# Comparisons of place in edge bucketing: six of the 34 rows made by ScalarE as a rectified one less the squared distance

## The chip, the cores and the metric

The kernel runs on one core of a Trainium2 chip. The metric is the device time of one execution in microseconds; the time of a kernel is the median of its runs. In the profile PE is TensorE (PEld its weight loads), DVE is VectorE, ACT is ScalarE, POOL is GpSimd, and SP is the engine that issues most DMAs.

## The reference

Four graph layers follow one another on 6250 nodes with 96 features and 100000 edges (`src`, `dst`, sorted by `dst`), each as x + layer(relu(layernorm(x))): four-head attention over edges, a softmax-weighted sum of messages, ten steps of a propagation, and two graph convolutions. All of them sum over edges by node. The cut below shows the shape of the work.

```python
edge_index = jnp.stack([src, dst])
h = jnp.maximum(_layernorm(x, axis=-1), 0.0)
x = x + _L0_gnn_ref(h, L0_gnn_qW, L0_gnn_kW, L0_gnn_vW, src, dst)   # exp(q.k) weights, segment_sum by src
h = jnp.maximum(_layernorm(x, axis=-1), 0.0)
x = x + _L1_gnn_ref(h, src, dst, L1_gnn_W, L1_gnn_b)                # softmax over dst, segment_sum, linear
h = jnp.maximum(_layernorm(x, axis=-1), 0.0)
x = x + _L2_gnn_ref(h, edge_index)                                   # ten times: out = A out * 0.9 + h * 0.1
h = jnp.maximum(_layernorm(x, axis=-1), 0.0)
x = x + _L3_gnn_ref(h, edge_index, L3_gnn_W1, L3_gnn_b1, L3_gnn_W2, L3_gnn_b2)
```

## The kernel before

The kernel turns the edge list into a dense adjacency matrix in tiles of 128 nodes, and does every sum over edges as a matmul. Its stages in time are: loads and the first norm; **bucketing** of the edges (`bucket_edges`); attention together with the writing of the adjacency; then the dense layers, which stream the adjacency back and are the rest of the span.

Bucketing, the stage that is changed, runs over 25 groups of 256 destination nodes. A group has its edges in 128 partitions of `RUN` = 34 each ("rows" r = 0 to 33, handled in 17 pairs, `TWOS_RUN`). For each edge it finds the rank among the edges of the group that have the same source tile (49 tiles), and puts the edge's code in the slot (rank, tile). One turn of the loop does this:

- PE, `tensor_rank` (L944): 83 small matmuls sum the rank of each edge of group g in the bank `rank_ps` (`pr`, 34 columns). 49 of them take the slices of `prod`, one for each tile.
- ACT (L979) copies `pr` into `rank`, as bf16.
- DVE, `vector_place` (L862): compares `rank` with 0 to 127 and writes the one-hot `onerank`, 128 columns for each of 34 rows. It does so in three instructions, of 6, 6 and 5 pairs, and signals `hot_r` after each.
- PE, `tensor_place` (L954): 34 matmuls, `onerank` of a row against `vals` of it, summed in `po`. It waits for `hot_r` before rows 0, 12 and 24 (`third` = 12), and signals `placed`.
- ACT (L990) copies `po` into the column g of `placed`, and signals `slots_out`.

Around this lie, for the group after it, the counting (`tensor_count`, L930, and ACT's copy of it, `before`, L984, which DVE's `prod`, L852, needs) and the projection of two node tiles to q, k, v: PE transposes (L623), ACT copies them to `aT` (L631), PE multiplies (`q_out`, L639), ACT takes the high half (L652) and DVE the low half (L659).

The order on each engine is that of the program. A turn is on PE: rank of g, count and transposes of g + 1, place of g, products of g + 1. On ACT: `rank`, `before`, `aT`, `placed`, then the two high halves. On DVE: `prod`, `bt`, `near`, `far`, `vals`, two low halves, three of `onerank`. Turn 20 also loads the Exp table on ACT, in turn 21 DVE decodes the first 20 groups (`decode(0)`, L805 to L815), and turn 25, the last, has place only.

Of the kernel before, what the change touches and what calls it, by code (L numbers as in the profile page):

```python
# [5 lines left out]
ALU = mybir.AluOpType  # L6
ACT = mybir.ActivationFunctionType
AX = mybir.AxisListType
F32, F16, BF16, F8 = mybir.dt.float32, mybir.dt.float16, mybir.dt.bfloat16, mybir.dt.float8e4
I32, U16, U8 = mybir.dt.int32, mybir.dt.uint16, mybir.dt.uint8  # L10

P = 128
# [5 lines left out]
GROUPS = -(-NODES // GROUP)  # L18
# [3 lines left out]
RUN = 34  # L22
# [15 lines left out]
EARLY = (CHUNKS - 1) * CHUNK  # L38
TURN = (6, BTILES // 2)
BANK = 4  # L40
AHEAD = 3
UP = -(-GROUPS // BANK)
HOMES = 5
# [70 lines left out]
def over(ap, n):  # L114
    return ap.unsqueeze(2).to_broadcast([ap.shape[0], ap.shape[1], n])
# [14 lines left out]
def signals(k):  # L130
    k.spare = k.sig("spare")
    k.const_raw, k.consts, k.ident_b = k.sig("const_raw"), k.sig("consts"), k.sig("ident_b")
    k.x_zero, k.dall_in, k.x_in, k.params_in = (k.sig(x) for x in ("x_zero", "dall_in", "x_in", "params_in"))
    k.below, k.first_ps, k.first, k.edges_in, k.edges_in2 = (
        k.sig(x) for x in ("below", "first_ps", "first", "edges_in", "edges_in2"))
    k.ln_x, k.ln_sum, k.ln_mean, k.ln_cen, k.ln_sq, k.ln_var, k.ln_vare, k.ln_std, k.ln_rstd, k.ln_h = (
        k.sig(x) for x in ("ln_x", "ln_sum", "ln_mean", "ln_cen", "ln_sq", "ln_var", "ln_vare", "ln_std", "ln_rstd",
                           "ln_h"))
    k.lin_tr, k.lin_copied, k.lin_mm, k.lin_out = (k.sig(x) for x in ("lin_tr", "lin_copied", "lin_mm", "lin_out"))
    k.x_plus, k.q_unit, k.q_unit_ps, k.q_root, k.q_scaled, k.q_per, k.q_hi, k.q_lo = (  # L140
        k.sig(x) for x in ("x_plus", "q_unit", "q_unit_ps", "q_root", "q_scaled", "q_per", "q_hi", "q_lo"))
    k.bound_in, k.eps_in = k.sig("bound_in"), k.sig("eps_in")
    k.rows_t, k.rows_sb, k.kv_zero = (k.sig(x) for x in ("rows_t", "rows_sb", "kv_zero"))
    k.rows_out = [k.sig(f"rows_out{h}") for h in range(2)]
    k.prepared = k.sig("prepared")
    k.bt, k.val, k.counted, k.before, k.same, k.prod, k.ranked, k.rank, k.hot_r, k.placed, k.slots_out = (
        k.sig(x) for x in ("bt", "val", "counted", "before", "same", "prod", "ranked", "rank", "hot_r", "placed",
                           "slots_out"))
    k.codes, k.decoded, k.planes = k.sig("codes"), k.sig("decoded"), k.sig("planes")
    k.base1, k.full_s, k.full_ps, k.filled_s = (k.sig(x) for x in ("base1", "full_s", "full_ps", "filled_s"))  # L150
    attention_signals(k)
    k.most_s, k.most_ps, k.verdict = (k.sig(x) for x in ("most_s", "most_ps", "verdict"))
# [528 lines left out]
def bucket_edges(k, ctx, edges, projection):  # L681
# [23 lines left out]
    far = [k.buf(ctx, f"far{i}", [P, 2, FAR, 2 * FAR], BF16) for i in range(2)]  # L705
    before = [k.buf(ctx, f"before{i}", [P, TILES, 2], BF16) for i in range(2)]
    rank = k.buf(ctx, "rankb", [P, RUN], BF16)
    onerank = k.buf(ctx, "onerank", [P, TWOS_RUN, P, 2], BF16)
    placed = k.buf(ctx, "placed", [P, BTILES, GROUPS], BF16)
    parts = ((0, EARLY), (EARLY, GROUPS))  # L710
# [14 lines left out]
    pr = k.bank(ctx, "rank_ps")  # L725
    pp = [k.bank(ctx, f"pp{i}") for i in range(2)]
    po = k.bank(ctx, "po")
    third = 2 * -(-TWOS_RUN // 3)
    tile1 = tile0[:, :, RUN:]

    def in_twos(row, n):
# [11 lines left out]

    def vector():
        v.tensor_scalar(count0_2[:], over(k.count1[:], 2), 1.0, None, ALU.subtract)
        v.tensor_copy(number_2[:], over(k.count1[:, 0:TILES], 2))
        v.tensor_copy(identh[:], k.ident[:])
        v.memset(placed[:, TILES:BTILES, :], 0.0)
        starts.count()
        starts.place()  # L750
        for turn in range(BODIES + AHEAD):
            if turn < BODIES:
                norm.center(turn)
            if turn == 0:
                projection.squares()
            elif turn == 1:
                projection.roots()
            elif turn == AHEAD:
                projection.units()
            if turn >= AHEAD:  # L760
                norm.scale(turn - AHEAD)
        prepare()
        for turn in range(GROUPS + 1):
            if turn:
                vector_before(turn - 1)
            if turn < GROUPS:
                vector_count(turn)
            if turn:
                projection.low(turn - 1)
                if turn == GROUPS:  # L770
                    planes(0)
                vector_place(turn - 1)
            if turn == EARLY + 1:
                decode(0)
        decode(1)
        planes(1)
        v.wait_ge(k.full_ps.sem, k.full_ps.at(1))
        v.tensor_reduce(k.filled[:], pc[0:1, 0:2], AX.X, ALU.add).then_inc(k.filled_s.sem, 1)
# [76 lines left out]
    def vector_place(g):  # L855
        v.wait_ge(k.rank.sem, k.rank.at(g + 1))
        if g:
            v.wait_ge(k.placed.sem, k.placed.at(g))
        ranks = in_twos(rank[:], P)
        for r0 in range(0, TWOS_RUN, third // 2):  # L860
            r1 = min(r0 + third // 2, TWOS_RUN)
            v.tensor_tensor(onerank[:, r0:r1, :, :], count0_2[:].unsqueeze(1).to_broadcast([P, r1 - r0, P, 2]),  # L862
                            ranks[:, r0:r1, :, :], ALU.is_equal).then_inc(k.hot_r.sem, 1)

# [54 lines left out]
    def copy_rows(h, n0, n1, m):  # L919
        first = h * n_early  # L920
        a.wait_ge(k.rows_t.sem, k.rows_t.at(first + n1))
        a.activation(flat(k.slot_rows[0:m, first + n0:first + n1, :]), pt[h][0:m, 0:(n1 - n0) * P],
                     ACT.Copy).then_inc(k.rows_sb.sem, 1)
# [23 lines left out]
    def tensor_place(g):  # L947
        pe.wait_ge(k.val.sem, k.val.at(g + 1))
        if g:
            pe.wait_ge(k.slots_out.sem, k.slots_out.at(g))  # L950
        for r in range(RUN):
            if r % third == 0:
                pe.wait_ge(k.hot_r.sem, k.hot_r.at(3 * g + r // third + 1))
            t = pe.matmul(po[:, 0:TILES], onerank[:, r // 2, :, r % 2], vals[g % 2][:, r // 2, :, r % 2],  # L954
                          start=r == 0, stop=r == RUN - 1)
        t.then_inc(k.placed.sem, 1)

    def scalar():
        a.wait_ge(k.consts.sem, k.consts.at(1))
        a.activation(warm[:], k.ones[:, 0:1], ACT.Sqrt).then_inc(k.kv_zero.sem, 1)  # L960
        starts.load(a, range(0, BY_SCALAR), k.edges_in)
        a.wait_ge(k.eps_in.sem, k.eps_in.at(1))
        for turn in range(BODIES + 1):
            if turn < BODIES:
                norm.square(turn)
            if turn:
                norm.deviation(turn - 1)
            if turn == 1:
                projection.root()
        for i in range(2):  # L970
            a.activation(k.aT[i][D:D + 1, :].rearrange("o (j p) -> o j p", p=P), under(k.ones[D:D + 1, :], RING), ACT.Copy)
        a.wait_ge(k.x_plus.sem, k.x_plus.at(16 * BODIES))
        for turn in range(GROUPS + 1):
            g = turn - 1
            if turn:
                a.wait_ge(k.ranked.sem, k.ranked.at(g + 1))
                if g:
                    a.wait_ge(k.hot_r.sem, k.hot_r.at(3 * g))
                a.activation(rank[:], pr[:, 0:RUN], ACT.Copy).then_inc(k.rank.sem, 1)  # L979
            if turn < GROUPS:  # L980
                a.wait_ge(k.counted.sem, k.counted.at(turn + 1))
                if turn >= 2:
                    a.wait_ge(k.prod.sem, k.prod.at(turn - 1))
                a.activation(before[turn % 2][:], over(pp[turn % 2][:, 0:TILES], 2), ACT.Copy).then_inc(k.before.sem, 1)  # L984
                projection.copy(turn)
            if turn == EARLY:
                a.activation(warm[:], k.ones[:, 0:1], ACT.Exp).then_inc(k.kv_zero.sem, 1)
            if turn:
                a.wait_ge(k.placed.sem, k.placed.at(g + 1))
                a.activation(placed[:, 0:TILES, g:g + 1], po[:, 0:TILES].unsqueeze(2), ACT.Copy).then_inc(k.slots_out.sem, 1)  # L990
            if turn < GROUPS:
                projection.high(turn)
            i = turn - EARLY - 1
            if 0 <= 8 * i < n_early:
                n1 = min(8 * i + 8, n_early)
                copy_rows(0, 8 * i, n1, EARLY * min(TURN[0], BTILES - 4 * i * TURN[0]))
        copy_rows(1, 0, 4, CHUNK * TURN[1])

    def spread(h, n0, n1):

# [1480 lines left out]
```

## Time and profile before

| | us |
|---|---|
| median of three runs | 3947.27 (3946.36 to 3948.25) |
| the profiled execution's own time | 3949.03 |
| its span | 3947.6 |
| PE busy | 3852.8 (98%) |
| DVE busy | 1728.5 (44%) |
| ACT busy | 1305.7 (33%) |
| one steady turn of bucketing | 6.88 |

A row of the timeline gives the start in us from the span's start, how long it took, the engine, the line, and in brackets how long that engine had been idle before and what ended the wait. The chain is the work that ended last, followed backwards; what lies on it sets the time.

### The profile page before, as it was taken

The numbers are of one execution on the slowest core, as the hardware profiler recorded it, in microseconds if no ns is written. First come the engines' busy times: TensorE is split into PE (matmuls) and PEld (weight loads), VectorE is DVE, ScalarE is ACT, GpSimd is POOL, SyncE is SP. The second block draws the span as 40 slices with busy tenths as digits, with TensorE's granted clock in tenths as the row PEclk, the third lists the DMA queues.
The fourth block names the chain that finished last, engine by engine and source line by source line (L and its number), as shares of the span: only waits on it lengthen the run. The fifth ranks groups of instructions, "written<-read, shape, count | busy, mean of one in ns | idle before, by whom it ended". The sixth has DMA issues, their size and how long they took to land.

```text
span 3947.6 us, 124895 instructions
## 1 busy us (share of the span) xinstructions
PE 3852.8 (98%) x46633; PEld 3664.5 (93%) x46633; DVE 1728.5 (44%) x4347; ACT 1305.7 (33%) x3974; POOL 589.7 (15%) x724
## 2 busy tenths in 40 slices
PE   5899999999999999999999999999999998999999
PEld 4789999999956668999999999999999998999999
DVE  8999999999963234222222222222222222331211
ACT  3268888888831012222221222212222221111110
POOL 1046666666610000000000000000000000000000
PEclk9999999999999999999999999999999999999999
DMA  3069898998953334566666565555655655666775
GB/s 66 3 170 231 232 239 232 233 236 231 239 162 112 112 106 156 205 201 205 202 203 204 200 205 201 203 204 200 205 201 202 204 201 175 207 218 209 213 214 157
DMA packets 441659, 750.12 MB, mean 190 GB/s; under 512 B 201515, under 2 KB 333227, under 8 KB 441496
## 3 DMA queue, kind: packets, MB, share of 16 engines
q1 hardware_dynamic: 438826, 744.71, 62.0%
q0 software_dynamic: 1232, 2.65, 0.4%
q8 instruction: 128, 2.10, 0.2%
q10 hardware_dynamic: 1438, 0.37, 0.0%
q14 instruction: 35, 0.29, 0.0%
HBM read 621.77 MB, written 83.32 MB: 179 GB/s over the span
## 4 chain that ended last, share of the span: by engine, by line
PE 95%; DVE 2%; issue 1%; SPq 1%; ACT 1%; DMA 0%; POOL 0%; DVEq 0%; ACTq 0%; POOLq 0%
PE sum L1939 50%; PE sum L1553 20%; PE pk L1274 10%; PE pr L1297 7%; PE pq L1286 3%; PE pc L1310 2%; PE rank_ps L944 2%; PE l L521 1%; DVE onerank L862 1%; PE q_out L639 1%; PE l L505 0%; PE sum L1764 0%; PE po L954 0%; SPq L288 0%; SPq L183 0%
## 5 line engine op out<-in xcount | busy, mean ns | idle before, releaser
L1939 PE MATMUL sum<-u,ring 128*128 128x192 f16 x12005 | 993.8, 246 | 0.0
L1939 PEld LDWEIGHTS sum<-u,ring 128*128 128x128 fp8e4 x12005 | 992.6, 98 | 0.8 <-issue 0.6
L1939 PE MATMUL sum<-y,ring 128*128 128x192 f16 x11662 | 962.9, 246 | 0.0
L1939 PEld LDWEIGHTS sum<-y,ring 128*128 128x128 fp8e4 x11662 | 962.2, 98 | 0.0
L1553 PE MATMUL sum<-u,ring 128*128 128x385 f16 (+1 forms) x4802 | 607.5, 287 | 7.6 <-issue 4.6
L1553 PEld LDWEIGHTS sum<-u,ring 128*128 128x128 fp8e4 x4802 | 435.1, 98 | 169.3 <-issue 8.0
L1948 DVE TENSOR_TENSOR z<-lo,sum 128x96 f32<-128x96 f32 x441 | 112.2, 254 | 988.6 <-ACT lo L1963 988.0
L1274 PE MATMUL pk<-kv,hT 128*128 128x192 f16 x4900 | 486.0, 246 | 2.0 <-DVE hT L1166 2.0
L1274 PEld LDWEIGHTS pk<-kv,hT 128*128 128x128 f16 x4900 | 410.1, 99 | 2.4 <-DVE hT L1166 2.3
L1356 ACT ACTIVATE kvs<-pk 128x384 f32<-128x384 f32 x735 | 302.6, 436 | 111.6 <-PE pk L1274 94.9
L1963 ACT ACTIVATE lo<-sum 128x96 f32<-128x96 f32 x441 | 110.1, 250 | 654.9 <-PE sum L1939 654.6
L1297 PE MATMUL pr<-wv,hs_wide 128*128 128x101 f32 x2450 | 322.4, 279 | 2.0 <-POOL wv L1227 2.0
L1222 POOL TENSOR_SCALAR sc<-sc,bound 128x20 f32<-128x20 f32 x245 | 263.3, 1075 | 258.1 <-DVE sc L1150 258.1
L1297 PEld LDWEIGHTS pr<-wv,hs_wide 128*128 128x128 f32 x2450 | 293.9, 192 | 2.3 <-POOL wv L1227 2.3
L1227 POOL TENSOR_TENSOR wv<-kvs,wv 128x480 f32<-128x480 f32 x245 | 246.8, 1007 | 208.8 <-DVE hd L1197 136.8
L1553 PE MATMUL sum<-y,ring 128*128 128x192 f16 x2401 | 202.2, 246 | 0.0
L1553 PEld LDWEIGHTS sum<-y,ring 128*128 128x128 fp8e4 x2401 | 199.0, 98 | 0.1
L1329 ACT ACTIVATE row<-pc 128x512 uint16<-128x512 f32 (+1 forms) x343 | 185.5, 545 | 0.8
L1346 ACT ACTIVATE hs_wide<-hs 128x640 f32<-128x640 bf16 x245 | 180.1, 735 | 0.0
L1143 DVE TENSOR_TENSOR qk<-pq,kvs 128x480 f32<-128x480 f32 x245 | 160.3, 654 | 42.0 <-ACT kvs L1356 42.0
L1951 DVE SCALAR_TENSOR_TENSOR uf<-z,col_g,H 128x96 f32<-128x96 f32 x441 | 140.6, 319 | 80.9 <-DVE z L1948 80.9
L1166 DVE TENSOR_SCALAR hT<-rows,dpid 128x640 f16<-128x640 f16 x490 | 165.9, 380 | 0.0
(257 smaller groups left out, 3018.3 us busy)
## 6 DMA issues: line engine op xcount, KB each, us to landing
ring<-adjacency_t SPq DMA_DIRECT2D x490, 800.0 KB, 4.3
ring<-adjacency SPq DMA_DIRECT2D x147, 896.0 KB, 5.0
rows<-slot_rows_d SPq DMA_DIRECT2D x249, 320.0 KB, 3.9
adjacency<-row SPq DMA_DIRECT2D x49, 800.0 KB, 4.3
adjacency_t<-col SPq DMA_DIRECT2D x49, 800.0 KB, 4.5
col<-row SPq DMA_TRANSPOSE x245, 4.1
X<-H POOLq DMA_DIRECT2D x7, 336.0 KB, 3.9
X<-in_x_dram SPq DMA_DIRECT2D x6, 336.0 KB, 5.4
```

What stands on the lines that cost most here:

```text
L1143: v.tensor_tensor(qk[i][:].rearrange("p (g d) -> p g d", d=D), pq[i][:, 0:CHUNK * D].rearrange("p (g d) -> p g d", d=D), kv[i][:, :, 0:D], ...
L1166: t = v.tensor_scalar(halves(hT[i][:, 1 + m, :, :]), halves(rows[h][:, :, 1, :]), k.dpid[:, m:m + 1], None, ALU.is_equal)
L1222: pool.tensor_scalar(sc[i][:], sc[i][:], k.bound[:, 0:1], k.bound[:, 1:2], ALU.min, ALU.max).then_inc(k.clipped.sem, 1)
L1227: pool.tensor_tensor(wv[i][:, :, 0:D].rearrange("p g (h d) -> p g h d", d=DH), kv[i][:, :, D:2 * D].rearrange("p g (h d) -> p g h d", d=DH ...
L1274: t = pe.matmul(pk[n][:, place:place + 2 * D], hT[i][:, 1 + m, g, :], k.kv[:, 2 * (g0 + g) + m, part, :], start=m == part == 0, stop=m == ...
L1297: t = pe.matmul(pr[:, 0:AV], hs_wide[e % HOMES][:, g, :], wv[i][:, g, :], start=g0 + g == 0, stop=g0 + g == GROUPS - 1)
L1329: a.activation(flat(row[b][:, g:g + count, :]), pc[u % 2][:, 0:count * P], ACT.Copy, accum_out=rowsum[:, bass.ds(X * (2 * UP) + u, 1)]).th ...
L1346: a.activation(flat(hs_wide[e % HOMES][:]), hs[e % 2][:].rearrange("p g a t -> p (g a t)"), ACT.Copy).then_inc(k.wide.sem, 1)
L1356: a.activation(flat(kv[i][:, 2 * n:2 * n + count, :]), pk[n][:, 0:count * 2 * D], ACT.Copy).then_inc(k.kv_out.sem, 1)
L1553: t = pe.matmul(self.ps[j][:, 0:self.cols], w[:, q, (j + odd) // 2, :, (j + odd) % 2], U[:, r * RING + q, 0:self.cols], start=r == q == 0, ...
L1939: m = pe.matmul(ps[r][:, 0:2 * D], w[:, t // 2, :, t % 2], n["this"][:, t, 0:2 * D], start=t == 0, stop=t == TILES - 1)
L1951: v.scalar_tensor_tensor(uf[j][:], z[:, j, :], k.g[:, tile], flat(k.H[:, tile, :]), ALU.mult, ALU.add).then_inc(k.uf.sem, 1)
```

## The change

For each group, ScalarE makes the comparisons of the last six rows (28 to 33, `BY_SQUARES` = 6, three pairs); VectorE makes the other 28 (`by_vector` = 14 pairs, in instructions of 5, 5 and 4 pairs, `third` = 10). ScalarE first copies the six columns of `pr` as f32 into `rank_f`, then makes six Square instructions, (rank - count)^2, each with its own column of `rank_f` as bias, into `away`; and, after `before`, one Relu of 1 - `away` over all six rows, which reads `away` with the two rows of a pair interleaved and writes `onerank` in order. The value is 1 where count equals rank, else 0. PE waits for the new signal `hot_a` before row 28. How `rank_ps` is summed (all 49 slices) stays.

```diff
+BY_SQUARES = 6
@@ bucket_edges
+    rank_f = k.buf(ctx, "rank_f", [P, BY_SQUARES], F32)
+    away = k.buf(ctx, "away", [P, BY_SQUARES, P], BF16)
+    count0 = k.buf(ctx, "count0", [P, P], BF16)
...
-    third = 2 * -(-TWOS_RUN // 3)
+    by_vector = TWOS_RUN - BY_SQUARES // 2
+    third = 2 * -(-by_vector // 3)
@@ vector()
+        v.tensor_scalar(count0[:], k.count1[:], 1.0, None, ALU.subtract)
@@ vector_place
-        for r0 in range(0, TWOS_RUN, third // 2):
-            r1 = min(r0 + third // 2, TWOS_RUN)
+        for r0 in range(0, by_vector, third // 2):
+            r1 = min(r0 + third // 2, by_vector)
@@ tensor_place
-            if r % third == 0:
+            if r == 2 * by_vector:
+                pe.wait_ge(k.hot_a.sem, k.hot_a.at(g + 1))
+            elif r % third == 0 and r < 2 * by_vector:
@@ scalar()
+                a.activation(rank_f[:], pr[:, 2 * by_vector:RUN], ACT.Copy).then_inc(k.rank_f.sem, 1)
                 a.activation(rank[:], pr[:, 0:RUN], ACT.Copy).then_inc(k.rank.sem, 1)
+                scalar_away(g)
...
+            if turn:
+                scalar_place(g)
+            if turn < GROUPS:
                 projection.copy(turn)
...
+    def scalar_away(g):
+        a.wait_ge(k.rank_f.sem, k.rank_f.at(g + 1))
+        for r in range(BY_SQUARES):
+            x = a.activation(away[:, r, :], count0[:], ACT.Square, bias=rank_f[:, r:r + 1], scale=-1.0)
+        x.then_inc(k.away.sem, 1)
+
+    def scalar_place(g):
+        a.wait_ge(k.away.sem, k.away.at(g + 1))
+        if g:
+            a.wait_ge(k.placed.sem, k.placed.at(g))
+        a.activation(onerank[:, by_vector:, :, :], away[:].rearrange("p (a t) n -> p a n t", t=2), ACT.Relu,
+                     bias=k.ones[:, 0:1], scale=-1.0).then_inc(k.hot_a.sem, 1)
```

On ACT, one steady turn of bucketing before, from the copy of the rank to the high halves of the projection:

```order
64 L979 ACTIVATE rankb<-rank_ps 128x34 [waits hot_r,ranked]
65 L984 ACTIVATE before<-pp 128x98 [waits prod,counted]
66 L631 ACTIVATE aT<-q_turned 96x256 [waits lin_tr,lin_mm]
67 L990 ACTIVATE placed<-po 128x49 [waits placed]
68 L652 ACTIVATE H<-q_out 128x2x96 [waits lin_mm]
69 L652 ACTIVATE kv<-q_out 128x2x192
```

The same turn of ACT in the changed kernel:

```order
76 L988 ACTIVATE rank_f<-rank_ps 128x6 [waits hot_r,ranked]
77 L989 ACTIVATE rankb<-rank_ps 128x34
78 L1017 ACTIVATE away<-count,rank_f 128x128 [waits rank_f]
79 L1017 ACTIVATE away<-count,rank_f 128x128 x5
80 L995 ACTIVATE before<-pp 128x98 [waits prod,counted]
81 L1024 ACTIVATE onerank<-away,ones 128x768 [waits placed,away]
82 L633 ACTIVATE aT<-q_turned 96x256 [waits lin_tr,lin_mm]
83 L1004 ACTIVATE placed<-po 128x49 [waits placed]
84 L654 ACTIVATE H<-q_out 128x2x96 [waits lin_mm]
85 L654 ACTIVATE kv<-q_out 128x2x192
```

Eight instructions are new: `rank_f` stands ahead of the copy of the rank, six squares stand ahead of `before`, and the Relu into `onerank` stands between `before` and `aT`.

On PE, the place matmuls of a turn and the products after them, before:

```order
15 L954 MATMUL po<-vals,onerank 128x49 [waits hot_r,val]
16 L954 MATMUL po<-vals,onerank 128x49 x11
17 L954 MATMUL po<-vals,onerank 128x49 [waits hot_r]
18 L954 MATMUL po<-vals,onerank 128x49 x11
19 L954 MATMUL po<-vals,onerank 128x49 [waits hot_r]
20 L954 MATMUL po<-vals,onerank 128x49 x9
21 L639 MATMUL q_out<-wq_scaled,aT 128x288 [waits q_lo,lin_copied]
```

And the same place of PE in the changed kernel:

```order
15 L963 MATMUL po<-vals,onerank 128x49 [waits hot_r,val]
16 L963 MATMUL po<-vals,onerank 128x49 x9
17 L963 MATMUL po<-vals,onerank 128x49 [waits hot_r]
18 L963 MATMUL po<-vals,onerank 128x49 x9
19 L963 MATMUL po<-vals,onerank 128x49 [waits hot_r]
20 L963 MATMUL po<-vals,onerank 128x49 x7
21 L963 MATMUL po<-vals,onerank 128x49 [waits hot_a]
22 L963 MATMUL po<-vals,onerank 128x49 x5
23 L641 MATMUL q_out<-wq_scaled,aT 128x288 [waits q_lo,lin_copied]
```

The last six of the 34 matmuls got a wait of their own, for ACT's `hot_a`; the products behind them wait for `aT` (`lin_copied`), as before.

## Rows read from the trace of the kernel before

**Rows 1.** Busy time of each engine in bucketing, and in one steady turn.

```profile
core 0: us, PE busy (x) PEld busy (x) DVE busy (x) ACT busy (x) POOL busy (x), PEclk, DMA share, GB/s
44.00:220.00 176.00, 153.81 (x3871) 134.85 (x3872) 168.72 (x256) 50.81 (x153) 0.00 (x0) 0.98 0.05 13
108.45:115.33 6.88, 6.11 (x165) 5.36 (x161) 6.70 (x11) 1.94 (x6) 0.00 (x0) 1.00 0.02 5
```

**Rows 2.** The chain that ended last, one turn: start us, us, what.

```profile
110.98 0.21 ACT rankb L979
...
112.96 0.83 DVE onerank L862
...
113.83 0.44 PE po L954 x10
114.27 1.06 PE q_out L639 x4
115.33 2.50 PE rank_ps L944 x83
```

**Rows 3.** The timeline of the same turn, DVE, ACT and PE.

```profile
110.98 0.20 ACT L979 ACTIVATE rankb<-rank_ps 128x34 bf16<-128x34 f32 x1 [1.78 <-PE rank_ps L944]
111.21 2.56 DVE L862 TENSOR_TENSOR onerank<-count,rankb 128x1536 bf16<-128x1536 bf16 x3 [0.18 <-ACT rankb L979]
...
111.87 0.25 ACT L984 ACTIVATE before<-pp 128x98 bf16<-128x98 f32 x1 [0.69 <-PE pp L930]
112.18 0.38 ACT L631 ACTIVATE aT<-q_turned 96x256 f32<-96x256 f32 x1
...
113.69 1.02 DVE L852 TENSOR_TENSOR prodb<-bt,before 128x1666 bf16<-128x1666 bf16 x1
113.83 0.33 PEld L954 LDWEIGHTS po<-vals,onerank 128*128 128x128 bf16 x10 [0.35 <-DVE onerank L862]
...
114.09 0.78 PEld L639 LDWEIGHTS q_out<-wq_scaled,aT 96*128 96x128 f32 x4
...
117.36 0.55 DVE L659 TENSOR_TENSOR kv<-q_out,kv 128x384 f16<-128x384 f32 x1
```

**Rows 4.** Groups by line and shape, 40 to 420 us: the comparisons on DVE.

```profile
L862 DVE TENSOR_TENSOR onerank<-count,rankb 128x1536 bf16<-128x1536 bf16 x50 | 45.7, 955 | 6.5 <-ACT rankb L979 6.5
...
L862 DVE TENSOR_TENSOR onerank<-count,rankb 128x1280 bf16<-128x1280 bf16 x25 | 20.5, 818 | 0.0
```

**Rows 5.** Groups of ACT by line and shape over the whole span.

```profile
L312 ACT ACTIVATE T<-H 128x672 f32<-128x672 f32 x21 | 16.0, 763 | 115.5 <-DVE H L307 115.5
...
L222 ACT ACTIVATE T<-H 128x96 f32<-128x96 f32 x49 | 13.1, 267 | 7.1 <-DVE H L215 7.1
...
L990 ACT ACTIVATE placed<-po 128x49 bf16<-128x49 f32 x25 | 9.8, 393 | 42.9 <-PE po L954 42.9
...
L979 ACT ACTIVATE rankb<-rank_ps 128x34 bf16<-128x34 f32 x25 | 5.0, 199 | 44.4 <-PE rank_ps L944 44.4
...
L228 ACT ACTIVATE col<-col,eps 128x7 f32<-128x7 f32 x7 | 1.9, 285 | 0.0
```

**Rows 6.** ACT's timeline in the first norm: two small instructions, back to back.

```profile
15.59 0.28 ACT L228 ACTIVATE col<-col,eps 128x7 f32<-128x7 f32 x1
15.78 0.19 ACT L592 ACTIVATE q_unitb<-q_unitb 128x3 f32<-128x3 f32 x1
```

**Rows 7.** The timeline of turn 0, where the products waited for `aT`.

```profile
43.76 0.38 ACT L631 ACTIVATE aT<-q_turned 96x256 f32<-96x256 f32 x1 [0.15 <-PE q_turned L623]
44.19 1.46 PEld L639 LDWEIGHTS q_out<-wq_scaled,aT 96*128 96x128 f32 x4 [0.90 <-ACT aT L631]
```

**Rows 8.** DVE's timeline at the start: one instruction that reads every 16th element.

```profile
5.17 0.21 DVE L262 CAST some<-dall 125x50 f32<-125x50 int32 x1 [0.35 <-DMA dall<-in_edges_dram]
```

**Rows 9.** The timeline of turn 21, behind `decode(0)`.

```profile
193.72 1.02 DVE L852 TENSOR_TENSOR prodb<-bt,before 128x1666 bf16<-128x1666 bf16 x1
...
194.81 0.53 PEld L944 LDWEIGHTS rank_ps<-near,identb 128*128 128x128 bf16 x16
```

**Rows 10.** The chain ahead of bucketing.

```profile
29.79 4.10 DMA edges<-in_edges_dram
```

More of the change, by code:

```diff
@@ L148, in signals @@
                            "slots_out"))
+    k.rank_f, k.away, k.hot_a = (k.sig(x) for x in ("rank_f", "away", "hot_a"))
     k.codes, k.decoded, k.planes = k.sig("codes"), k.sig("decoded"), k.sig("planes")
```

## The prediction

> **What bounds the kernel now.** I read the busy time by stretch first. In bucketing DVE is busy 168.72 of 176 us and PE 153.81, ACT only 50.81; in one steady turn of 6.88 us DVE works 6.70, PE 6.11, ACT 1.94 [rows 1]. So DVE looks like the bound and ACT has 4.9 us a turn to spare. Then the chain of waits, which says what a turn really hangs on [rows 2]: the 83 rank matmuls (2.50), ACT's copy of the rank (0.21), the three DVE comparisons, the last ten place matmuls (0.44), the products (1.06), and the rank matmuls again. Everything else of DVE fits beside this, with 0.18 us to spare: that is its idle time before `onerank` [rows 3]. So both a DVE instruction in `onerank` and an ACT or PE instruction between rank and products are on the path. Last the timeline of that turn [rows 3]. I call T the end of the rank matmuls (110.96, which is 0.02 ahead of ACT's copy) and give places as T plus so much: `rank` copied T+0.02 to T+0.22, `onerank` T+0.25 to T+2.81, `before` from T+0.91, `aT` T+1.22 to T+1.60, the last place weights at T+2.87, the products' first weights at T+3.13. From there to the next T is 6.88 - 3.13 = 3.75, work of PE alone that the change doesn't touch.
>
> **What comes off DVE.** Six pairs of rows take 0.955, five 0.818 [rows 4]: 0.137 a pair, and the three pairs that leave are worth 0.41 a turn. On the path that is the whole gain there is: 25 turns x 0.41 = 10.3 us, 0.26% of the kernel.
>
> **What comes ahead of the copy of the rank.** `rank_f` is a copy of 6 columns. ACT's price is a fixed part and 0.86 ns an element ((763 - 267) / (672 - 96), [rows 5]); 28 columns less than the 199 ns of `rank` make 0.175. Two ACT instructions overlap by 0.09: the one of 0.28 at 15.59 is followed at 15.78 [rows 6]. So `rank` starts 0.08 later, and `onerank` runs from T+0.33 to T+2.48. Of the 0.41 there is 0.33 left. The third DVE piece is now followed by 8 + 6 matmuls in place of 10, at 0.026 each (the ten take from 113.83 to 114.09, [rows 3]), which takes 0.10 more. If ACT's part were there in time, the products would start at T+2.90, 0.23 earlier than now.
>
> **What ACT has to do first.** A 128x96 Square takes 0.267 without a tensor as bias [rows 5]. A bias tensor costs about 0.09: 0.285 for 7 elements with one, 0.19 for 3 without [rows 5, 6]. So one square of 128 elements is 0.267 + 32 x 0.00086 + 0.09 = 0.385, and the next starts 0.295 after it. The squares start at T+0.21 (after `rank`), the last of six at T+0.21 + 5 x 0.295 = T+1.69, and it ends at T+2.07. `before`, due at T+0.91 now, starts at T+1.98 and ends at T+2.23. It is queued behind the squares, and DVE's `prod` waits for it, but `prod` stands behind `onerank`, which ends at T+2.48: covered by 0.25. The Relu starts 0.16 after `before`, at T+2.14. It does 768 elements with a bias tensor: 0.763 + 96 x 0.00086 + 0.09 = 0.94 if its read costs no more than a plain one, so `hot_a` comes at T+3.08. Behind it on ACT is `aT`, for which the products on PE wait: it starts at T+2.14 + 0.94 - 0.09 = T+2.99, takes 0.38, ends at T+3.37, and PE loads 0.05 after its end (43.76 + 0.38 to 44.19, [rows 7]). **Products at T+3.42**, against T+3.13: a steady turn gets 0.29 us longer, 7.17. The six last place matmuls (T+3.13 to T+3.29) hide under `aT`. DVE gets off the path (6.29 of 7.17 busy), PE waits more.
>
> **The price of the Relu's read** is what the trace doesn't show: it takes turns between two rows 256 bytes apart, and no ACT row here reads like that. Lower bound: the plain 0.94. Upper bound: the one ACT row whose access jumps, the 49 scattered elements of `placed`, at 0.393 [rows 5]; less a fixed 0.17 (199 ns less 34 x 0.86) that is 4.5 ns an element, and the Relu would be 768 x 0.0045 + 0.26 = 3.7 us. But there it is the write that jumps, while the Relu writes in order. A read that jumps is in one row, on DVE: 50 elements, each 64 bytes from the last, in 0.21 [rows 8], no more than such small instructions take anyway. It is the nearest row, so I take the plain price.
>
> In a sentence apart: the Trainium skill (SBUF — State Buffer, its note on cachelines) says that SBUF has lines of 16 bytes, that at least two hits in a line are needed for full bandwidth, and that each access that crosses to a new line pays; by that rule every element of this read pays, which is the second rival below, and the DVE row of 64-byte steps speaks against it (it shows another engine).
>
> **The turns that differ.** Turns 1 to 20, 22 and 23 are steady: 22 x 0.29 = 6.4. Turn 21 has `decode(0)` on DVE behind `onerank`, and PE's rank starts at 194.81, just after `prod` (193.72 + 1.02) [rows 9]: there DVE's 0.33 are a gain, and ACT's work is under the decode, -0.3. Turn 24 projects one tile, `aT` is 0.1 shorter: +0.2. Turn 25 has neither `before` nor `aT`; ACT ends at T+3.0, about when DVE's path did: 0. The `count0` instruction at the start is covered, since DVE then waits for a DMA of edges that lands at 33.9 [rows 10]. Attention after bucketing is untouched and starts as much later. Turn 20's table load stands behind `aT` and ahead of `placed`, where ACT has over a microsecond.
>
> **The sum:** 6.4 - 0.3 + 0.2 = +6.2 us (rounded), to be set against the profiled execution's own 3949.03, which gives 3955.3; that execution lies 1.8 over the median of the runs, so I state it against the median: 3947.27 + 6.2 = **3953.5**, 0.16% more. A measurement of this kernel can tell about 0.2% (7.9 us) from no change, so the forecast falls under "same", with 0.07 us a turn to the border.
>
> **Rivals.**
>
> *The intended gain.* If ACT's chain ends before DVE's, the products start at T+2.90. That needs `aT` by T+2.85, 0.52 sooner than I sum, so squares at an interval of 0.21 instead of 0.295, which would be so if the bias tensor cost nothing. Then it's 22 x -0.23, -0.3 in turn 21 and -0.4 in the last two: -5.8, **3941.5**. For it: 6.70 of DVE's 6.88 busy. Against it: the 0.285 for seven elements. Even this rival isn't over 0.2%.
>
> *The jumping read costs extra* (ends on the other side). Each 0.07 us more in the Relu makes the kernel measurably slower, since it is on the path in 24 turns (all but 21). At half speed, 0.86 ns more an element, the Relu takes 1.60, each turn 0.66 more: 6.2 + 24 x 0.66 = +22, **3969**. This is the likely form of the rule named above. For it: the alternation is with every element, and `placed` shows that ACT can pay for a jump. Against: the DVE row.
>
> *The jump costs what the write of `placed` does,* 3.7 us: 2.8 more in 24 turns, +67 and 6.2, **4021**. PE would wait 3 us a turn and might lose clock too. Against: it is a row of single 2-byte writes.
>
> *The change does less than it says* can't be: the order shows all eight new ACT instructions in each turn, and no further table load.
>
> **Chances.** Forecast (ACT's path ends last, plain read, +3 to +10) 0.55; the gain 0.12; extra read cost up to 1 us a turn 0.24; more 0.09. Of the forecast's 0.55 I give 0.15 to over 7.9 us, for small waits between dependent ACT instructions that I set at nothing (0.07 a turn decides). So faster by over 0.2%: 0.02, within 0.2%: 0.50, slower: 0.15 + 0.24 + 0.09 = 0.48. The range reaches from the gain to the half-speed read, 3941 to 3970; what is left out is the last case and the upper part of the third, about 0.15. The forecast's own range is 3950 to 3957.
>
> **What would show it.** In the changed profile: DVE comparisons of 1280 and 1024 columns, 2.15 in all; squares of 0.385 at intervals of 0.295; the Relu at 0.94 (its duration decides between forecast and second rival at once); `before` at T+1.98; products at T+3.42, released by ACT's `aT`; a steady turn of 7.17; DVE idle before `onerank` some 0.8 in place of 0.18. I am wrong if the Relu is far over 1 us, if the products are released by the place matmuls and not by `aT`, or if the whole differs from 24 times the change of a steady turn by more than 2 us, which would mean that something outside bucketing moved.

## The result, and the profile after

| | before | changed |
|---|---|---|
| median, us | 3947.38 (13 runs, 3945.36 to 3949.25) | 3956.73 (13 runs, 3954.23 to 3958.77) |
| ratio to before | | 1.0023, 95% interval 1.0015 to 1.0032 |
| the profiled execution's own time / its span | 3949.03 / 3947.6 | 3957.29 / 3954.0 |
| one steady turn of bucketing | 6.88 | 7.22 |

The kernel got slower by 9.3 us, 0.23%, where 6.2 us, 0.16%, were forecast. Timed once more on one chip beside the kernel before, it had 1.0022 (1.0013 to 1.0031).

Busy time of each engine in one steady turn of the changed kernel, from T to T (to be set against [rows 1]):

```profile
core 0: us, PE busy (x) PEld busy (x) DVE busy (x) ACT busy (x) POOL busy (x), PEclk, DMA share, GB/s
...
107.00:114.22 7.22, 6.39 (x164) 5.49 (x161) 6.29 (x10) 4.51 (x16) 0.00 (x0) 1.00 0.01 2
```

DVE does lose 0.41 a turn (6.70 to 6.29), ACT goes from 1.94 to 4.51, and the turn is 0.34 longer. ACT is still idle for 2.7 us of it: its busy share would never name it as the bound. The chain does. One turn of it in the changed kernel (start, us, what), to be set against [rows 2]:

```profile
114.14 0.18 ACT rank_f L988
114.32 0.07 ACT rankb L989
114.39 0.28 issue
114.66 0.40 ACT away L1017 x2
115.06 0.19 issue
115.25 0.97 ACT away L1017 x3
116.22 0.06 ACT before L995
116.27 1.01 ACT onerank L1024
117.29 0.05 issue
117.33 0.33 PE po L963 x6
117.67 1.17 PE q_out L641 x4
118.83 2.50 PE rank_ps L951 x83
```

DVE, which had three pieces of `onerank` on this path, isn't on it at all. In its place stand ACT's two copies, its squares, `before` and the Relu, 3.15 us from 114.14 to 117.29 (in the kernel before, ACT's copy and DVE's comparisons took 2.81, 110.98 to 113.79, [rows 2]). The same turn in the timeline (start, us, engine, line, operation, in brackets its idle time before; T is 114.12), to be set against [rows 3]:

```profile
114.14 0.18 ACT L988 ACTIVATE rank_f<-rank_ps 128x6 f32<-128x6 f32 x1 [1.78 <-PE rank_ps L951]
114.22 0.19 ACT L989 ACTIVATE rankb<-rank_ps 128x34 bf16<-128x34 f32 x1
114.35 1.87 ACT L1017 ACTIVATE away<-count,rank_f 128x128 bf16<-128x128 bf16 x6
114.44 2.16 DVE L869 TENSOR_TENSOR onerank<-count,rankb 128x1280 bf16<-128x1280 bf16 x3 [0.93 <-ACT rankb L989]
...
116.12 0.23 ACT L995 ACTIVATE before<-pp 128x98 bf16<-128x98 f32 x1
116.26 1.02 ACT L1024 ACTIVATE onerank<-away,ones 128x768 bf16<-128x768 bf16 x1
116.52 1.02 DVE L859 TENSOR_TENSOR prodb<-bt,before 128x1666 bf16<-128x1666 bf16 x1
116.66 0.27 PEld L963 LDWEIGHTS po<-vals,onerank 128*128 128x128 bf16 x8 [0.27 <-DVE onerank L869]
...
117.18 0.36 ACT L633 ACTIVATE aT<-q_turned 96x256 f32<-96x256 f32 x1
117.33 0.23 PEld L963 LDWEIGHTS po<-vals,onerank 128*128 128x128 bf16 x6 [0.40 <-ACT onerank L1024]
...
117.59 0.78 PEld L641 LDWEIGHTS q_out<-wq_scaled,aT 96*128 96x128 f32 x4
```

Three things are to be seen. DVE waits 0.93 before `onerank`, against 0.18. PE sits idle before the last six weights until ACT's Relu is done. And two chains end close together ahead of the products (117.59). `aT` ends at 117.18 + 0.36 = 117.54, 0.05 before them. The six place weights begin at 117.33; at 0.026 from one start to the next, as in [rows 3], PE would be free for the products at 117.49. So it's `aT` by 0.10, though the chain above goes through the place matmuls: the profile models a matmul's end, and takes PE as busy until then. The second experiment below takes the two apart.

### The profile page after: what moved, and what is told of

It reads as the page before. It is cut to its first block, busy times and chain, and to the rows that moved or that the text cites. A ratio compares the mean times of both kernels' runs of the same rounds, so it can differ in the third digit from the quotient of the medians.

```text
span 3954.0 us, 125120 instructions
## 1 busy us (share of the span) xinstructions
PE 3857.6 (98%) x46633; PEld 3665.5 (93%) x46633; DVE 1717.4 (43%) x4348; ACT 1371.4 (35%) x4174; POOL 599.9 (15%) x724
## 4 chain that ended last, share of the span: by engine, by line
PE 95%; ACT 2%; DVE 2%; issue 1%; SPq 1%; DMA 0%; POOL 0%; DVEq 0%; ACTq 0%; POOLq 0%
PE sum L1967 49%; PE sum L1581 20%; PE pk L1302 10%; PE pr L1325 7%; PE pq L1314 3%; PE pc L1338 2%; PE rank_ps L951 2%; ACT away L1017 1%; PE l L523 1%; PE q_out L641 1%; ACT onerank L1024 1%; PE l L507 0%; PE sum L1792 0%; SPq L290 0%; PE po L963 0%
## 5 line engine op out<-in xcount | busy, mean ns | idle before, releaser
L1250 POOL TENSOR_SCALAR sc<-sc,bound 128x20 f32<-128x20 f32 x245 | 279.1, 1139 | 265.2 <-DVE sc L1178 265.2
```

Of the source, the lines that this page charges most:

```text
L1250: pool.tensor_scalar(sc[i][:], sc[i][:], k.bound[:, 0:1], k.bound[:, 1:2], ALU.min, ALU.max).then_inc(k.clipped.sem, 1)
```

## The experiments

All start from the changed kernel unless said otherwise. The measure is the steady turn, the distance between two copies of the rank in the timeline; in each profile turns 2 to 20 repeat it within 0.02 us, except for some turns of two kernels in which PE's granted clock fell. Those two are the kernel with one square more and the one with the rank copied first, and their figures are those of the turns at full clock. Where a whole time of one run is given, runs of one kernel differ by up to 5 us, so small differences between such times say nothing.

**One square more.** Into an unused tile.

```diff
         for r in range(BY_SQUARES):
+            if r == 0:
+                a.activation(idle[:], count0[:], ACT.Square, bias=rank_f[:, 0:1], scale=-1.0)
             x = a.activation(away[:, r, :], count0[:], ACT.Square, bias=rank_f[:, r:r + 1], scale=-1.0)
```

> The changed kernel with one more Square of the same form into an unused tile, ahead of the six. Theory A (ACT's chain is on the path): the turn grows by the whole interval of a square, 0.295, to 7.51. Rival C (PE or DVE ends last and ACT has slack): 7.22 to 7.25.

Measured: 7.51 (112.28 to 119.80, and again 7.51). All of the 0.295 lands on the turn: ACT has no slack, though it idles a third of the time. The whole time, 3967.0, isn't used, because something else is in it: 5 of the first 20 turns took 7.88 to 8.37, at a mean granted clock of 0.78 to 0.80, where it is 1.00 in the other fifteen. One of them began at 104.00 and took 8.28; busy times before and inside it:

```profile
core 0: us, PE busy (x) PEld busy (x) DVE busy (x) ACT busy (x) POOL busy (x), PEclk, DMA share, GB/s
99.75:107.30 7.55, 6.38 (x157) 5.48 (x157) 6.43 (x11) 4.84 (x17) 0.00 (x0) 1.00 0.01 2
107.30:109.70 2.40, 2.30 (x20) 1.59 (x20) 2.40 (x5) 0.76 (x4) 0.00 (x0) 0.66 0.00 0
109.70:112.20 2.50, 2.50 (x87) 2.50 (x84) 1.07 (x3) 0.66 (x2) 0.00 (x0) 0.65 0.04 10
```

**ACT's new work done, but waited for by nobody.** DVE makes all 34 rows again, in pieces of 6, 6 and 5 pairs; PE waits for `hot_r` alone; ACT's Relu writes an unused tile. In the second form the Relu stands behind `aT`.

```diff
-    third = 2 * -(-by_vector // 3)
+    third = 2 * -(-TWOS_RUN // 3)
...
-        a.activation(onerank[:, by_vector:, :, :], away[:].rearrange("p (a t) n -> p a n t", t=2), ACT.Relu,
+        a.activation(idle[:], away[:].rearrange("p (a t) n -> p a n t", t=2), ACT.Relu,
... second form only:
+            if turn < GROUPS:
+                projection.copy(turn)
             if turn:
                 scalar_place(g)
-            if turn < GROUPS:
-                projection.copy(turn)
```

> VectorE makes all 34 rows and PE waits for VectorE alone, in three pieces of 6, 6 and 5 pairs as in the kernel before; ACT does all of its new work at the same places, but into an unused tile, so nobody waits for hot_a. Theory A1 (the queue is what costs: aT stands behind the Relu on ACT and the products wait for it): products at T+3.47 as in the changed kernel, turn 7.22. Rival A2 (the wait for hot_a and the six matmuls behind it is what costs): DVE's path, 0.08 later than before because of rank_f, turn 6.96.

> As the kernel in which ACT's new work goes into an unused tile and VectorE makes all rows, but the Relu stands behind aT instead of ahead of it. Theory A1 (the queue ahead of aT costs): aT ends near T+2.5, before DVE's path, and the turn is 6.96, the 6.88 of before and 0.08 for rank_f ahead of the copy of the rank. Rival (ACT's work costs even where nothing on the path is queued behind it, by sharing memory or by delaying before and placed): 7.0 or more.

Measured: 7.22 with the Relu ahead of `aT`, 6.95 with it behind. The timeline of the first form, where DVE's comparisons and place are done by 117.3 and PE still waits, now with ACT's `aT` named as the releaser:

```profile
116.15 1.02 ACT L1023 ACTIVATE idle<-away,ones 128x768 bf16<-128x768 bf16 x1
...
117.08 0.36 ACT L633 ACTIVATE aT<-q_turned 96x256 f32<-96x256 f32 x1
...
117.49 0.78 PEld L641 LDWEIGHTS q_out<-wq_scaled,aT 96*128 96x128 f32 x4 [0.21 <-ACT aT L633]
```

So the queue alone costs the whole 0.34: with no wait for `hot_a` at all the turn is what it was in the changed kernel. Put behind `aT`, the same work costs only 0.07 a turn, and that is `rank_f` ahead of the copy of the rank: `onerank` starts at T+0.32 in place of T+0.25. (The whole time of its one run was 3951.8 against 3948.3; 1.1 us of that lies outside the span, on which see the end.) ACT's work isn't dear in itself. Its place in ACT's order is. In the changed kernel itself, moving `aT` ahead of the Relu would by the same numbers not help: the Relu would be pushed back by 0.27, and the six place matmuls behind it end only 0.10 before `aT` does. That is argued; the order was not run.

**The Relu reads its rows in order.** It writes a tile of its own, from which PE takes the last six weights.

```diff
-        a.activation(onerank[:, by_vector:, :, :], away[:].rearrange("p (a t) n -> p a n t", t=2), ACT.Relu,
+        a.activation(oneplain[:], away[:], ACT.Relu,
...
+            hot = onerank[:, r // 2, :, r % 2] if r < 2 * by_vector else oneplain[:, r - 2 * by_vector, :]
```

> The changed kernel, but the Relu writes a tile of its own, row by row, so that it reads away in order (PE takes its last six weights from that tile). If the turns between two rows cost ACT something, the Relu falls from the 1.02 us measured to the 0.94 that I summed from plain rows, and the turn, which hangs on it, from 7.22 to 7.14. If they cost nothing, Relu and turn stay at 1.02 and 7.22.

Measured: Relu 0.930, turn 7.13. All instructions of the Relu in this kernel, and in the changed one (duration in ns: min/median/max):

```profile
L1026 ACT ACTIVATE oneplain<-away,ones x25: 928/930/937, 51.5 to 226.2; 128x768 bf16<-128x768 bf16 x25
```

```profile
L1024 ACT ACTIVATE onerank<-away,ones x25: 1017/1022/1023, 51.3 to 228.1; 128x768 bf16<-128x768 bf16 x25
```

The jumping read does cost, 0.09 us for 768 elements or 0.12 ns each. That is real and on the path, and it is far from the rival's half speed. The rule of the Trainium skill that I had weighed (SBUF — State Buffer, its note on cachelines: each access that crosses to a new line pays) has the sign right; here the price is a tenth of the instruction. That such lines are its cause isn't shown by these runs.

**The rank copied ahead of `rank_f`.**

```diff
-                a.activation(rank_f[:], pr[:, 2 * by_vector:RUN], ACT.Copy).then_inc(k.rank_f.sem, 1)
                 a.activation(rank[:], pr[:, 0:RUN], ACT.Copy).then_inc(k.rank.sem, 1)
+                a.activation(rank_f[:], pr[:, 2 * by_vector:RUN], ACT.Copy).then_inc(k.rank_f.sem, 1)
```

> The changed kernel with the two copies of the rank sums in the other order (rank first, then rank_f; the rank matmuls of the next group wait for both). Theory A (a steady turn hangs on ACT's own chain of squares, before, Relu and aT): the comparisons on DVE start 0.08 us earlier, but nothing waits for them; the squares wait for rank_f, which now ends 0.1 later, so the turn stays at 7.22 or gets up to 0.1 longer (7.31). Rival B (the turn hangs on the DVE comparisons, begun later because of rank_f): 7.14.

Measured: 7.31 in 16 of the first 20 turns; the other four took 7.59 to 8.04, at a mean granted clock of 0.78 to 0.79. The comparisons start 0.07 earlier after T and nothing comes of it; the squares start 0.09 later, after `rank_f`, and the turn takes all of that. What helps DVE's chain hurts ACT's: the order must be chosen for the chain that ends last.

**Fewer rows on ACT.** `BY_SQUARES` = 4 and 2.

> The changed kernel with four rows on ACT instead of six (30 rows on DVE, pieces of 5, 5 and 5 pairs). Theory A (two chains side by side, the later sets the turn): ACT's ends 0.81 earlier (two squares of 0.295, 256 elements less in the Relu), products could start at T+2.66; DVE's chain: 0.33 + 15 x 0.137 + 0.24, then 14 matmuls, T+3.05. Turn 6.80, below the kernel before by 0.08. Rival (each row on ACT costs in proportion): 6.88 + 4/6 of 0.34 = 7.11.

> The changed kernel with two rows on ACT (32 on DVE, pieces of 6, 6 and 4 pairs). Theory A: ACT's chain is far ahead; DVE's chain ends one pair later than with four rows (0.137) but leaves 10 matmuls instead of 14 (0.10 less): products at T+3.08, turn 6.82. Rival (proportional): 6.88 + 2/6 of 0.34 = 6.99.

Measured: 6.785 with four rows, 6.81 with two (3946.4 and 3945.2 in one run each, before 3948.3). The turn goes 6.88, 6.81, 6.79, 7.22 with 0, 2, 4 and 6 rows: two chains side by side, flat while DVE's is the later one and then steep. It doesn't go in proportion. With four rows the chain is DVE's again; PE has 14 matmuls left behind the last piece:

```profile
113.78 0.83 DVE onerank L869
114.61 0.05 issue
114.65 0.55 PE po L963 x14
115.20 1.06 PE q_out L641 x4
116.26 2.51 PE rank_ps L951 x83
```

That is where the rest of the gain went. Two pairs less on DVE are 0.27, but `rank_f` takes 0.07 back, and four more matmuls behind the last piece (14 in place of 10) another 0.1.

**The kernel before with its pieces cut 7, 7 and 3.** No ACT work at all; only the matmuls behind the last piece change.

```diff
-    third = 2 * -(-TWOS_RUN // 3)
+    cuts = (0, 7, 14, TWOS_RUN)
...
-            if r % third == 0:
-                pe.wait_ge(k.hot_r.sem, k.hot_r.at(3 * g + r // third + 1))
+            if r % 2 == 0 and r // 2 in cuts:
+                pe.wait_ge(k.hot_r.sem, k.hot_r.at(3 * g + cuts.index(r // 2) + 1))
```

> The kernel before with the comparisons cut into pieces of 7, 7 and 3 pairs instead of 6, 6 and 5. If the path runs through DVE's last piece and the place matmuls behind it, six matmuls are left instead of ten: 4 x 0.026 = 0.10 us less, turn 6.78. If DVE's own work (6.70 of 6.88 busy) or PE's matmuls of the second piece bind first, 6.80 to 6.88.

> The kernel before with pieces of 7, 7 and 3 pairs, timed. Its turn was 6.77 in one profile, 0.11 less: 24 x 0.11 = 2.6 us, a ratio of 0.9993; if the gain of bucketing is lost behind it, 1.0.

Measured: a turn of 6.77. Timed: 3945.01 against 3947.30, ratio 0.9995 (0.9986 to 1.0004). The turn is as expected; the 2.3 us of the medians are too few to be told from nothing. The turn is as short as with four rows on ACT (6.79), without one new instruction.

**Both put right.** Four rows on ACT, the rank copied first, and PE takes ACT's rows ahead of DVE's last piece. DVE's pieces are 5, 5, 5 in one kernel and 6, 6, 3 in the other (shown).

```diff
-BY_SQUARES = 6
+BY_SQUARES = 4
...
+    cuts = (0, 6, 12, by_vector)
...
+        last = 2 * cuts[2]
+        order = [*range(last), *range(2 * by_vector, RUN), *range(last, 2 * by_vector)]
+        for n, r in enumerate(order):
```

> The same with DVE's pieces of 5, 5 and 5 pairs: ten matmuls are left behind the last piece in place of six. Theory A: 4 x 0.026 = 0.10 us a turn more than with 6, 6 and 3, turn 6.61, 6.5 us less than the kernel before (0.9984). If the turn is the same 6.5 as with uneven pieces, the matmuls behind the last piece are not on the path.

> Four rows on ACT, the rank copied ahead of rank_f, and PE takes ACT's four rows ahead of DVE's last piece; DVE's pieces are 6, 6 and 3 pairs, so six matmuls are left behind the last. Theory A (two chains; the later one plus what PE has left sets the turn): DVE's last piece ends at T+2.54, products at T+2.76; ACT's aT is ready at T+2.73; turn 6.51, -0.37 in 23 turns and -0.3 in turn 21: 8.8 us less than before, a ratio of 0.9978. Rival (DVE's own work or ACT's chain binds first, or PE with 0.3 us of waiting left): 6.6 or more, a ratio over 0.9985.

Measured: turns of 6.61 and 6.50. The kernel with 5, 5, 5 takes 3941.11 (ratio 0.9985, 0.9976 to 0.9994), the one with 6, 6, 3 takes **3938.18** (11 runs), against 3947.30 for the kernel before on the same chip: **0.9977** (0.9968 to 0.9986). It beats both kernels. The 0.11 us a turn between the two forms is the short last piece. Copying the rank first and taking ACT's rows early came together (6.785 to 6.61) and were not run apart. One turn of the faster form in the timeline (T is 107.96):

```profile
107.98 0.20 ACT L990 ACTIVATE rankb<-rank_ps 128x34 bf16<-128x34 f32 x1 [1.78 <-PE rank_ps L951]
...
108.21 2.30 DVE L868 TENSOR_TENSOR onerank<-count,rankb 128x1536 bf16<-128x1536 bf16 x3
...
109.59 0.78 ACT L1026 ACTIVATE onerank<-away,ones 128x512 bf16<-128x512 bf16 x1
110.09 0.69 PEld L965 LDWEIGHTS po<-vals,onerank 128*128 128x128 bf16 x22 [0.42 <-DVE onerank L868]
...
110.27 0.37 ACT L633 ACTIVATE aT<-q_turned 96x256 f32<-96x256 f32 x1
110.42 1.02 DVE L859 TENSOR_TENSOR prodb<-bt,before 128x1666 bf16<-128x1666 bf16 x1
...
110.71 0.78 PEld L641 LDWEIGHTS q_out<-wq_scaled,aT 96*128 96x128 f32 x4
```

The Relu is done at 110.37, before DVE's last piece (110.51); PE runs 22 place weights without a stop; `aT` ends at 110.64, and the products start at T+2.75 in place of T+3.13. The Relu, DVE's last piece and `aT` end within 0.3 us of one another. DVE is busy for 6.42 of 6.50, so this is near the end of what moving rows about can give.

**The changed kernel once more,** for how its 9.3 us divide.

> The changed kernel once more, beside the kernel before on one chip, for how the difference splits into the span and the time around it. From its first profiles: turn 7.22, span 6 to 8 us longer; the rest of the 9.3 us by which the medians differ would be outside the span. If the span differs by all of it, nothing is outside.

Measured: medians 3956.67 against 3947.30, that is 9.4. The median span is 3953.6 against 3945.6 (8.0); the time around the span 3.1 against 1.7 (1.4).

## Why the prediction was right, and where it was short

The path, its cause and its sign were right, and the time lies in the range (3941 to 3970). The forecast's own range, 3950 to 3957, held it too, but only by 0.3 us, and the measured time has 1.4 us in it for which the forecast had no term. The sum has a slip as well: 6.4 - 0.3 + 0.2 is 6.3, not 6.2. Point by point:

- **DVE's gain** of 0.41 a turn, 0.33 after `rank_f`: right. `onerank` runs from T+0.32 to T+2.48 (T+0.33 to T+2.48 forecast).
- **The squares**: T+0.23, six in 1.87 (T+0.21 and 1.86 forecast). The price of a bias tensor, taken from an instruction of seven elements, held at 128. `before` came at T+2.00 and the Relu at T+2.14, as worked out.
- **The Relu's read**: I took the plain price, 0.94, and it was 1.02. The plain price itself was right (0.93 with the read in order); that the jump costs nothing was not. The DVE row I had relied on [rows 8] was no proof for ACT, and 0.09 us was below what one row of 0.21 could have shown. The rival at half speed is out.
- **"The six last place matmuls hide under aT"**: right, by 0.10 where I had 0.13. But the test that I named for it was a bad one. I wrote that I'd be wrong if the products were "released by the place matmuls and not by `aT`", and the chain does name the place matmuls. Only with the wait for `hot_a` gone did the trace name `aT`, at the same turn of 7.22: two releasers this close have to be parted by their starts, not by the name in the chain.
- **The steady turn**: 7.22, 7.17 forecast. The products start at T+3.47 in place of T+3.42, the Relu's 0.08 in the main. This is the mis-sized term: 22 x 0.34 = 7.5 in place of 6.4.
- **The other turns**: turn 21 gave back 0.35 (0.3 forecast), turn 24 took 0.10 (0.2), the last turn took 0.16 (0). The first matmul of attention came 7.75 later (226.79 and 234.54), 0.25 more than the end of bucketing: PE waits for `hT` on DVE, and DVE had waited 0.31 before it. SP issued the row loads that `hT` reads 7.7 later (213.64, then 221.36), which fits; that they are the cause was not tested.
- **What I hadn't in the sum at all**: 1.4 us outside the span. With it, 8.0 + 1.4 makes the 9.4. My test of 24 times the change of a steady turn, 8.2, passed at 9.3 because it allowed 2 us.
- **The border**: I gave 0.48 to "slower by over 0.2%" and 0.50 to "the same" with 0.07 us a turn between them. The turn came 0.05 longer and the rest did it, at 0.23%.

## What to carry to other kernels

Work given to an idle engine costs by where it stands in that engine's order, not by how busy the engine is: ask what is queued behind it and who waits for that (here the Relu stood ahead of a copy that PE needed, 0.34 us a turn, and behind that copy the same work cost 0.07). When two engines share a job, write both chains to the point where they meet, and move work only until they end together: four rows made the turn shorter, six made it longer. And count what the consumer has left to do behind the last piece; with four rows, the order alone (rank copied first, helper's rows taken early, a short last piece) gave 0.28 of the 0.38 us a turn that the best kernel won. The uneven cut needs no new instruction: by itself it took 0.11 off the turn of the kernel before.

## What was not expected of the hardware

- A Relu of 768 bf16 elements that takes turns between two rows 256 bytes apart took 1.022 us, and 0.930 reading in order. With 512 and 256 elements it took 0.776 and 0.527, so 0.97 ns an element.
- PE's granted clock fell in some turns of the two kernels whose turns are the longest, and in none of turns 1 to 20 of the others (steady turns of 7.22 or less): 4 of 20 with the rank copied first, 5 of 20 with one square more. Against the steady turns of their kernels these took 1.9 and 3.1 us more in all. In the turn of 8.28 shown above the granted clock was 0.50 (1.2 GHz) from 108.1 to 111.5 us, and the products in it took 1.94 us in place of the 1.24 of the next turn. PE had waited 0.57 us for ACT's Relu just before, but it does so in the next turn too, which ran at 1.00. So PE's rows of these two turns don't show what parts them, and that the longer turn is the cause isn't shown.
- The time outside the span was longer in some kernels than in others. In the changed kernel it was 2.9 to 3.4 us in all 11 runs of its second timing, and 2.1 to 3.4 (median 3.1) in the 13 of its first, beside 1.5 to 2.0 in the 33 of the kernel before. It was about 3 in four of its variants (rank first, plain Relu, and both with an unused Relu); it was 1.5 to 2.1 in the kernels with four and two rows, and also with a seventh square, which has more instructions than any of them. Nothing in the traces shows the cause, and it stays open. It is worth 1.4 us, a seventh of this result, and no row of a span can forecast it.
